# Multiplying the edge basis in fp32 in row tiles of 32 lanes, instead of in stacked bfloat16 parts, in a two-layer graph network

## The reference

```python
# layer 0
s_n, v_n = _equiv_layernorm(s, v, gamma_s, beta_s, gamma_v)
msg_s = (s_n @ Ws_src)[src] + (s_n @ Ws_dst)[dst]      # msg_v likewise
w1 = rbf @ W_rbf                                       # (edges, 16) x (16, 224)
m1_s, m1_v = _cg_tp(msg_s, msg_v, y0, y1, w1[:, :64], ...)   # products with w1 and harmonics
# attention logits from m1_s, softmax over the edges of a target, gated values, segment sum
# layer 1
...                                                    # silu(basis @ Wfc1 / 4) @ Wfc2 -> 192 weights per edge
...                                                    # products with gathered rows, segment sum, norm
```

## Time and profile before

| | |
|---|---|
| runs | 7517.89, 7512.8, 7546.15 us; median 7517.89 |
| profiled execution | 7512.8 us, span 7512.8 us |
| PE busy | 6722.4 us (89%) |
| DVE busy | 6803.0 us (91%) |
| ACT busy | 5146.0 us (68%) |
| POOL busy | 5146.0 us (68%) |
| first transpose to last copy of `prepare` | 26.4 to 262.1 us |
| `edges` | 285 to 4345 us |
| `edges1` | 5328 to 7333 us |

### The profile page before, as it was taken

The page is one execution under the profiler, slowest core; times in us unless marked ns, Lnnn a source line. Parts: engine busy times, 40 slices in busy tenths (PEclk is TensorE's granted clock), DMA queues, the critical chain, the costliest instruction groups (busy, mean ns, idle before and its releaser), DMA issues. The chain is left out here.

```text
span 7512.8 us, 193248 instructions
## 1 busy us (share of the span) xinstructions
PE 6722.4 (89%) x44602; PEld 5295.6 (70%) x44603; DVE 6803.0 (91%) x15442; ACT 5146.0 (68%) x16654; POOL 5146.0 (68%) x5264
## 2 busy tenths in 40 slices
PE   7588899999989899898999839999899999999997
PEld 4388888888888888888888839996455555555556
DVE  8599999999999999999999978877699999999997
ACT  3277777777777777777777711116688888888884
POOL 3377777777777777777777729860477777777760
PEclk6699999999999999999999969998899999999998
DMA  6454444444444444444444418765455555555556
GB/s 203 126 110 108 108 110 108 110 108 110 108 108 110 108 110 108 110 108 108 109 108 110 104 63 254 224 181 96 114 141 142 142 142 143 142 141 142 142 134 197
DMA packets 971093, 967.50 MB, mean 129 GB/s; under 512 B 452030, under 2 KB 788030, under 8 KB 970942
## 3 DMA queue, kind: packets, MB, share of 16 engines
q0 software_dynamic: 225792, 385.65, 22.6%
q1 hardware_dynamic: 511312, 346.34, 17.1%
q10 hardware_dynamic: 233936, 234.90, 9.4%
HBM read 677.51 MB, written 288.65 MB: 129 GB/s over the span
## 5 line engine op out<-in xcount | busy, mean ns | idle before, releaser
L718 POOL DMA_INDIRECT e_g_src<-table_src,e_idx x1568 | 1542.0, 983 | 505.0 <-issue 477.8
L718 POOL DMA_INDIRECT e_g_dst<-table_dst,e_idx x1568 | 1499.8, 957 | 478.0 <-issue 417.6
L1929 POOL DMA_INDIRECT f_e<-table,f_src x1568 | 1494.5, 953 | 465.7 <-issue 441.4
L755 PE MATMUL e_ps_t<-ident,e_m 128*128 128x128 f32 (+1 forms) x7840 | 1149.9, 277 | 405.3 <-DVE e_m L975 401.2
L1988 PE MATMUL f_ps_a<-sums 128*128 128x384 f32 x3936 | 1402.0, 499 | 1.5 <-DVE sums L2088 1.5
L755 PEld LDWEIGHTS e_ps_t<-ident,e_m 128*128 128x128 f32 (+1 forms) x7840 | 865.1, 139 | 528.9 <-issue 468.7
L1988 PEld LDWEIGHTS f_ps_a<-sums 128*128 128x128 f32 x3936 | 707.7, 190 | 504.7 <-issue 90.3
L848 ACT ACTIVATE e_m1t<-e_ps_t 128x512 f32<-128x512 f32 (+1 forms) x1176 | 692.7, 595 | 337.1 <-PE e_ps_t L755 214.8
L781 PE MATMUL e_ps_v<-e_w_v,e_m1t 128*128 128x64 f32 x3136 | 649.4, 289 | 0.0
L812 PE MATMUL e_ps_h<-e_w_h,e_m2t 96*128 96x96 f32 x3136 | 648.8, 289 | 0.0
L811 PEld LDWEIGHTS e_ps_h<-e_w_h,e_m2t 128*128 128x128 f32 x3136 | 507.0, 191 | 189.9 <-issue 189.2
(11 more groups left out here) (270 smaller groups left out, 16566.3 us busy)
## 6 DMA issues: line engine op xcount, KB each, us to landing
edge_values<-e_h ACTq DMA_DIRECT2D x392, 330.0 KB
r_h<-edge_values SPq DMA_DIRECT2D x196, 660.0 KB, 4.1
sums<-sums ACTq DMA_DIRECT2D x492, 192.0 KB
e_g_src<-table_src,e_idx POOLq DMA_INDIRECT x1568
e_g_dst<-table_dst,e_idx POOLq DMA_INDIRECT x1568
f_e<-table,f_src POOLq DMA_INDIRECT x1568
f_rbf<-basis SPq DMA_DIRECT2D x492, 48.0 KB
basis<-t_part SPq DMA_DIRECT2D x42, 448.0 KB, 3.1
```

What stands on the lines that cost most here:

```text
L718: pool.indirect_dma_start(out=into[:, r, t, :], out_offset=None, in_=table, in_offset=bass.IndirectOffsetOnAxis(ap=idx[:, r, c:c + 1], axi ...
L755: last = nc.tensor.transpose(ps_t[bank][0:channels, t * P:(t + 1) * P], rows(t), ident[:])
L1929: pool.indirect_dma_start(out=rows_of_units[:, (place * RING + r) * T + t, :], out_offset=None, in_=table, in_offset=bass.IndirectOffsetOn ...
```

## The change

The basis stays fp32. `prepare` only normalises and multiplies the nodes; the basis tensor in memory is gone, and both passes load from the input.

In `edges`, the 512 edges of a unit are held as two halves of 256 columns, the first in lanes 0 to 15, the second in lanes 32 to 47. `W_rbf` stands twice, in the same lanes. Each of the four fp32 matmuls takes 16 rows, and neighbours in the list are in different tiles of 32 rows. In `edges1` the 512 edges are held as four quarters of 128 columns in lanes 0, 32, 64 and 96 onwards, `Wfc1` stands four times, and there are four matmuls with 64 result columns each. Its result tile is one tile over two banks, where before two tiles alternated; the wait on `silu` is one step closer for that reason.

```diff
+LANES = 32
+BASES = 16
+def load_basis(engine, into, rbf_d, at, sem):
+    size = into.shape[1]
+    for k in range(GROUP // size):
+        engine.dma_start(into[k * LANES:k * LANES + BASES, :], rbf_d[:, bass.ds(at + k * size, size)]).then_inc(sem, 16)
...
 # prepare: SP, GpSimd and VectorE
-                wait(sp, left, (c - 2) * 2 + 1)
-                sp.dma_start(piece[:, r, :], whole[:, bass.ds(at, size)]).then_inc(piece_in[r], 16)
-                store_parts(c - 1, 1 - r, at_last)
                 store(c - 2, r)
...
-            whole_part(0, 0, 0)
-            in_pairs_to_last(pool, chunks, body)
...
-                dve.wait_ge(rounded, parted(c))
-                nc.vector.tensor_tensor(remain[:, r, :], piece[:, r, :], part[:, r, 0, :],
-                                        ALU.subtract).then_inc(left, 1)
...
-                dve.wait_ge(rounded, c * 3 + 2)
-                nc.vector.tensor_tensor(remain[:, r, :], remain[:, r, :], part[:, r, 1, :],
-                                        ALU.subtract).then_inc(left, 1)
...
 # edges
-            sp.wait_ge(parted, 5)
-            stack_weight(sp, parts_rbf, stack_rbf, stacked)
...
             def radial_weights(u, r, i):
-                pe.wait_ge(rbf_in[r], (i + 1) * 16 * len(PARTS_OF_PAIRS))
+                pe.wait_ge(rbf_in[r], (i + 1) * 32)
                 wait(pe, first, u * FIRST)
-                for t in range(T):
-                    last = nc.tensor.matmul(radial_w[:, t, 0:WN],
-                                            rbf[:, r, t * P:(t + 1) * P], stack_rbf[:], start=True, stop=True)
+                for n in range(T // 2):
+                    for half in range(2):
+                        lanes = slice(half * LANES, half * LANES + BASES)
+                        last = nc.tensor.matmul(radial_w[:, half * 2 + n, 0:WN], rbf[lanes, r, n * P:(n + 1) * P],
+                                                w_rbf[lanes, :], start=True, stop=True)
                 last.then_inc(radial, 1)
...
-            split_weight(nc, dve, w_rbf[:], rest_rbf[:], parts_rbf, parted)
...
 # edges1
-        ps_h = [ctx.enter_context(nc.psum_tensor(f"f_ps_h{i}", [P, 512], F32)) for i in range(2)]
+        ps_h = ctx.enter_context(nc.psum_tensor("f_ps_h", [P, 1024], F32))
+        inner = ps_h[:].rearrange("p (n k) -> p n k", n=2)[:, :, 0:P]
...
-                pe.wait_ge(rbf_in[r], (i + 1) * 16 * len(PARTS_OF_PAIRS))
-                wait(pe, silu, s - 1)
-                for half in range(2):
-                    last = nc.tensor.matmul(ps_h[r % 2][half * CS:(half + 1) * CS, 0:HALF], stack_1[:],
-                                            rbf[:, r, half * HALF:(half + 1) * HALF], start=True, stop=True)
+                pe.wait_ge(rbf_in[r], (i + 1) * 16 * T)
+                wait(pe, silu, s)
+                for t in range(T):
+                    half, n = divmod(t, 2)
+                    lanes = slice(t * LANES, t * LANES + BASES)
+                    last = nc.tensor.matmul(inner[half * CS:(half + 1) * CS, n, :], w_1[lanes, :], rbf[lanes, r, :],
+                                            start=True, stop=True)
                 last.then_inc(hid, 1)
```

More of the change, by code:

```diff
@@ L296, in sem @@
             return ctx.enter_context(nc.semaphore(f"t_{n}"))
-        piece, remain = sb("piece", [P, 2, size]), sb("remain", [P, 2, size])
-        part = sb("part", [P, 2, 3, size], BF16)
         x = sb("x", [P, 2, CHUNK, D])
@@ L364, in store @@
                 sp.dma_start(dv[c], o[:, r, :, D:2 * D]).then_inc(stored[r], 16)
-            def store_parts(c, r, at):
-                if isinstance(c, int) and c < 0:
-                    return
-                sp.wait_ge(rounded, c * 3 + (4 if not isinstance(c, int) or c < chunks - 1 else 3))
-                sp.sem_inc(issued, 1)
-                for k in range(3):
-                    rows = basis_d[k * bases:(k + 1) * bases, :].rearrange("k (a n) -> (k a) n", a=lines)
-                    sp.dma_start(rows[:, bass.ds(at, size)], part[:, r, k, :]).then_inc(parts_out[r], 16)
             def body(c, r, j):
-                at, at_last = column(sp, c), column(sp, c - 1)
                 wait(sp, own, (c - 1) * NORMED)
                 sp.dma_start(x[:, r], xv[c]).then_inc(loaded[r], 16)
-                wait(sp, left, (c - 2) * 2 + 1)
-                sp.dma_start(piece[:, r, :], whole[:, bass.ds(at, size)]).then_inc(piece_in[r], 16)
-                store_parts(c - 1, 1 - r, at_last)
                 store(c - 2, r)
             in_pairs(sp, chunks, body)
-            store_parts(chunks - 1, 1, column(sp, chunks - 1))
             store(chunks - 2, 0)
@@ L2009, in activate @@
                 wait(act, radial, s - 1)
-                nc.scalar.activation(hidden[:, r % 2, :], ps_h[r % 2][:, 0:HALF], ACT.Silu,
+                nc.scalar.activation(hidden[:, r % 2, :].rearrange("p (n k) -> p n k", n=2), inner, ACT.Silu,
                                      scale=1.0 / math.sqrt(16.0)).then_inc(silu, 1)
@@ L2377, in message_passing @@
         middle(nc, xn, sums0, factor, table1, resid, idx, sources, sources_in, w, w1, ident)
-        edges1(nc, idx, harmonics, basis, table1, *rows, until_row, sources, sources_in, w1, iota, sums0, sums1, issued)
+        edges1(nc, idx, harmonics, rbf, table1, *rows, until_row, sources, sources_in, w1, iota, sums0, sums1, issued)
         final(nc, sums1, factor, resid, out, w1, ident)
```

96 lines of the change are left out of this document (20 added, 76 removed).

## The result

| | before | changed |
|---|---|---|
| median of 7 runs, us | 7517.89 (7512.0 to 7551.23) | 7584.35 (7566.55 to 7613.98) |
| profiled execution, us (span) | 7512.8 | 7569.34 (7567.4) |

What follows compares the result with a forecast made beforehand. TensorE's low clock and pauses were taken to limit the first stage, GpSimd the first edge pass, VectorE the second. -85 + 25 + 12 - 11 = -59 us from 7512.8 gave 7454, 7459 in the median; range 7415 to 7565.

Steps and rivals of the forecast that it cites:

- First stage: Stage normalising and multiplying nodes: pauses go, clock rises after 45 us, 151 us against 235.7; -85 us, bounds -35 and -100.
- rival B: First stage's clock stays low: -35 us there, -9 in all, 7509 us in the median; chance 0.22.
- Its 0.60: Mean granted clock read for the first stage before the change, with 235.7 us for 14 chunks, 16.8 us each.
- The middle stage: Unchanged stage, taken as model for the first stage's clock: 0.50 for 45 us, then 1.00 for 163 us.
- First pass: First edge pass: radial matmul +0.63 us a unit, loop 10.19 us, level with GpSimd; +25 us, bounds 0 and +314.
- The 0.06 us for irregular units: First edge pass: added because nothing averages out for free; 0.06 x 392 = +25 us.
- Rival C: 32-lane tiles do not overlap in either edge pass: +551 us, 8069 us; chance 0.07.
- Second pass: Second edge pass: hidden layer 0.42 us, TensorE's turn 4.04 against VectorE's 4.02; +12 us, bounds nothing and +333.
- Rival D: Second pass's four hidden-layer tiles run only in twos: 0.64 us, +118 in place of 12, 7565 us; chance 0.14.
- Starts: Starts of both edge passes: stacking of the split weights goes; about -5 and -6 us, together -11.

Runs made afterwards that it cites:

- e2: Changed kernel with the first edge pass's radial matmuls placed behind the last block of transposes; ratio 1.0264, first pass 7065 us, low clock in the passes.
- e4: Changed kernel with 60 unused fp32 matmuls on the identity before the first stage's stream; ratio 1.0146, middle stage 338.4 us.
- e5: Same kernel as e2, run again on another chip; ratio 1.0295, first pass 7070 us.
- e8: The changed kernel itself, on a chip with the lower clock in the passes; 12219.84 us, ratio 1.0183.
- e9: Changed kernel with the first pass's fp32 radial matmuls all in one row tile; ratio 1.0365, 1.71 us a unit against 0.96.
- e6: Changed kernel, first-stage root one block earlier, one more fp32 matmul a block, 70 idle matmuls before the middle stage; ratio 1.0117, first stage 149.4 us.
- e7: e6 with 22 more idle matmuls ahead of the second chunk's first transpose in the middle stage; ratio 1.0121, middle stage 314.4 us.
- e11: Changed kernel with only the first stage edited: root one block earlier, one more fp32 matmul a block; ratio 1.0112, first stage 148.3 us.
- e13: e11's first stage together with e2's later radial matmuls, full-clock chip; 8128.34 us, ratio 1.0762, first pass 4737 us.
- e14: e11 again, on the same full-clock chip as e13; 7507.64 us, ratio 0.9959.
- e1: Changed kernel with the first stage's square root asked for one block earlier; ratio 1.0134, first stage 191.2 us.
- e12: Kernel before, first-stage root one block earlier and three more fp32 matmuls a block; 7532.08 us, ratio 1.0006, first stage 236.7 us.
- e10: Kernel before with only the second edge pass changed to fp32 in four row tiles; ratio 1.008, second pass 3791 us.
- e3: Kernel before with only the first edge pass changed to fp32 in row tiles; ratio 1.0113, first pass 6926 us.

## Why the prediction was wrong

**First stage: the step that failed.** "Without pauses I expect the same as in the middle: 45 us low, then 10.9 chunks at the pace of VectorE." Three things in it were wrong.

- The pauses did not go. At the low level a wait that the splitting had covered came up behind it: the root, asked of ScalarE after the fifth block. It cost 0.83 us in each of 13 chunks, and I had compared only the sums of busy time, VectorE's 9.7 against TensorE's 14.6. At the high level the pause was in the forecast's own numbers: 8.1 us of TensorE against a pace of 9.7 leave it standing for 1.6 us in each chunk. The forecast also said that a high spell lasts until the next pause, and still let the level stand for 10.9 chunks.
- The level did not stay. In the six profiles that have the changed kernel's order in this stage (its own, e2, e4, e5, e8, e9) it rose by itself 24 times before the last chunk, first 11 to 177 us after the first block, and fell 24 times at a change of chunk, 1.8 to 4.1 us after TensorE had begun a pause of 1.1 to 2.4 us there. With one more small fp32 matmul in each block and the root one block earlier, TensorE needs 9.7 us a chunk at the high level and pauses 0.59 us; the level was up 5 to 12 us after the first block and outlived all 61 such pauses, in five profiles (e6, e7, e11, e13, e14: 147 to 149 us). So for this stage rival B (-35 us) was the case. The pieces that decide are e1 and e11: same order, same root, and only the added matmul between 191 and 148 us.
- Why the added matmul works is not settled. It shortens the pause at the high level (2.4 us in the changed kernel, 1.3 in e1, 0.59 with it), and it makes the stream denser; one of e1's two pauses of 1.26 us and one of 1.30 in e12 cost no level. No run brings that pause under 1.26 us without adding matmuls to each block.
- The middle stage was no witness. Half of its blocks have the first stage's shapes, the other half (the averaged ones) multiply by half as many columns, and its high spell meets no pause until the last chunk. It comes up when it happens to: 39 to 224 us after its first block in the profiles where it is unchanged, and falls at the one long pause that it has then, of 4.34 us. I had taken one draw, 45 us, for its behaviour.

That 151 us were forecast for the high level and 147 to 149 were measured is in part luck: the forecast had 45 us at the low level and then 9.7 us a chunk, and the runs had 5 to 12 us and then 10.4.

The row of the middle stage was weighed against the Trainium skill, "TensorE: Matmul & The Clock Gate", Part 4 (PE-mode transpose), by which the full clock does not engage for transposes, and I followed the row. The runs do not bear the page out as a rule: streams of which half are transposes came up by themselves in every profile, in the middle stage for 72 to 178 us at a time. It agrees with them that the first stage was low for most of its time and that ordinary matmuls added to it went with the high level.

The reading of the stage before was at fault too. Its 0.60 was 0.54, as said above, and it was not TensorE's block and a pause that set 16.8 us a chunk, but the loop through the pieces of the basis (e12). With the split, a higher clock gave nothing.

**The middle stage: a term that was missing, and is chance as far as these runs show.** In the 14 profiles in which it is unchanged it takes 257.6 to 338.4 us, with a mean of 279. The one of before was 16 us under that and the one of the changed kernel 14 over. The longest and one of the short ones, each from TensorE's first block there to its last, e4 and e14:

```profile
7948.70:8262.90 314.20, 308.94 (x1176) 213.04 (x1176) 171.44 (x258) 154.53 (x406) 0.00 (x0) 0.61 0.35 72
```
```profile
5041.80:5278.00 236.20, 225.31 (x1155) 159.88 (x1154) 168.92 (x252) 147.34 (x400) 0.00 (x0) 0.87 0.44 99
```

The work is the same (1176 matmul rows; some records are missing in the second), the clock is not. This chance belongs into the range of any forecast for this kernel, and mine had no room for it. Without it the profiles differ by 54.6 - 29.9 = 25 us, at the lower end of the measured interval (24 to 64 us). What makes up the rest of the 44 us (or of the 66 between the medians) is not settled; the profiled execution of before was among the fastest of its seven, and such chance in the first stage and the middle may be all of it.

**First pass: right mechanism, size off.** The loop was named as it is: cross product, transposes, radial matmuls, transposes, ScalarE, vy. Forecast 3.26 + 0.63 = 3.89, then 0.1, then 6.20; measured 3.97 + 0.12 + 6.21 = 10.30 us. The mis-sized term is the radial matmul: it takes 0.96 us to the next transpose, less than the 1.02 that I gave it, but it also begins later. Behind the start of the transposes it starts after 0.59 us (2006.28 to 2006.87), where the bf16 one did after 0.48 (to 2008.97 in the earlier trace rows, from this line of the kernel before):

```profile
2008.49 0.65 PE L755 MATMUL e_ps_t<-ident,e_m 128*128 128x128 f32 x4 [1.22 <-DVE e_m L975]
```

The change costs time on both sides of the radial matmul, and I had counted one: 0.57 + 0.11 = 0.68 of the 0.71 us, where I had 0.63. The 0.06 us for irregular units was also the wrong sort of term: with this loop as the bound the units are regular. 391 x 0.12 = 47 us, where I had 25. The loop is read from the time line; the one run that took the radial matmuls out of it at the full clock, e13, put a longer loop in its place. Rival C, no overlap, is out by e9.

**Second pass: right.** 0.38 us for the hidden layer against 0.42, a turn of 4.01 against 4.04. The mean step went up by 20.2 / 491 = 0.04 us, where I had 0.02 to 0.03: TensorE's 4.01 is a floor under each of its steps, and VectorE's long steps (4.1 to 4.4 us) are not made shorter by the time that it gains. Rival D, tiles in twos, had 0.64 us and is out. The Trainium skill, "TensorE: Matmul & The Clock Gate", Part 3 (measured speedup), with 3.07 for four row tiles, was weighed there too: by it the estimate was 0.49 us, by the row 0.42, and 0.38 were measured.

**Starts.** -5.5 and -5.9 us, where -5 and -6 were forecast.

A first pass in four row tiles was not tried.

## What to carry to other kernels

Before an edit removes the bound of a stage, write its loop out to the end, with each engine's order, not only the busy times: what the removed work had covered (here a root, one block too late) is the next wait. If a stage of small matmuls and transposes runs at the low clock, look at whether TensorE bounds it at all. If it does, work out what TensorE will wait for once its clock is high: here it outran VectorE by up to 2.4 us a chunk, and every spell at the high level of the changed kernel's first stage ended there. One idle fp32 matmul a block where it would wait anyway, with the root one block earlier, was worth 65 us for 98 added matmuls. Read the level from the durations of the instructions too, since a row's granted clock says nothing of the time ahead of the first change. A stage whose clock comes up by chance has no length but a spread, and needs several profiles before one is used in a sum.

## What the hardware showed besides

The chip that ran e5 at 11998 us for the kernel before ran it at 7537 for e13. While the clock was low in the passes, TensorE also stood still for long stretches, here for 16 us in the second pass of e8:

```profile
8516.90 2.85 PE L1904 MATMUL f_ps_a<-sums 128*128 128x384 f32 x8
8535.72 0.70 PE L1880 MATMUL f_ps_h<-f_rbf,f_w 16*64 16x128 f32 x8 [15.97 <-ACT f_hidden L1926]
```

It waits there for ScalarE, and ScalarE's activation had waited 18.92 us for something that the profile does not name. ScalarE has 68 such waits, 930 us in all, before this activation from 8500 to 11500 us. So the clock is not all that differs on these chips, and which of the two comes first is not shown. There the change cost 1.8% instead of 0.6: first pass 6806 to 6970 us (e10, e8, one chip), second pass 3706 to 3787 (e3, e1, one chip). That what is added to TensorE counts more there fits, and is not shown. And e13 shows that another order of the same matmuls, with waits of 0.53 and 0.27 us a unit in place of one of 0.65, can bring the clock down on a chip that kept it at 1.00 for the first order; why, no run here tells. Of its 72 falls 66 had no pause over 0.76 us before them, so the pauses that ended the high spells of the first stage are not the only way to lose the level.
